# Four graph layers on one core: the statistics of x moved to the ranking loop, and three of eight source one-hots given to VectorE

## The reference

```python
h = jnp.maximum(_layernorm(x, axis=-1), 0.0)
x = x + _L0_gnn_ref(h, src, dst, ...)      # degrees of src and dst, h * norm_src @ W1, sums over edges, twice
...
# layer 0
deg_out = segment_sum(ones, src); deg_in = segment_sum(ones, dst)
norm_src, norm_dst = rsqrt(max(deg_out, 1)), rsqrt(max(deg_in, 1))
h = x * norm_src[:, None] @ W
agg = segment_sum(take(h, src), dst)
return agg * norm_dst[:, None] + b
```

## Time and profile before

| | us |
|---|---|
| median of 3 runs | 5414.27 (5409.69 to 5419.62) |
| the profiled execution | 5407.06, span 5405.3 |
| counting loop | 43 to 381 |
| ranking loop | 422 to 921 |
| first walk over the edges | from 994 |

### The profile page before, as it was taken

The page is one execution under the profiler, slowest core; times in us unless marked ns, Lnnn a source line. Parts: engine busy times, 40 slices in busy tenths (PEclk is TensorE's granted clock), DMA queues, the critical chain, the costliest instruction groups (busy, mean ns, idle before and its releaser), DMA issues. The chain is left out here.

```text
span 5405.3 us, 128432 instructions
## 1 busy us (share of the span) xinstructions
PE 4108.1 (76%) x23475; PEld 3077.4 (57%) x23476; DVE 3370.8 (62%) x11882; ACT 2977.7 (55%) x6277; POOL 3087.2 (57%) x3244
## 2 busy tenths in 40 slices
PE   3556777677668887677479999997888357777777
PEld 1124444477557776666467777776777245555555
DVE  6887776566357775677433333336877337777777
ACT  6974554377446665677433333335766236556556
POOL 0006776477765575767643345535567577777771
PEclk9899999899889998788689999999999669999999
DMA  2223333377545554788544444446888456666664
GB/s 74 76 61 92 104 104 94 117 218 217 165 139 168 167 182 147 225 266 269 170 130 135 135 136 143 145 141 216 275 277 274 143 146 201 200 199 202 202 197 148
DMA packets 599046, 905.03 MB, mean 167 GB/s; under 512 B 98280, under 2 KB 253680, under 8 KB 598956
## 3 DMA queue, kind: packets, MB, share of 16 engines
q1 hardware_dynamic: 456314, 646.24, 35.7%
q0 software_dynamic: 100352, 180.83, 13.7%
q10 hardware_dynamic: 42290, 77.00, 4.3%
HBM read 491.22 MB, written 412.49 MB: 167 GB/s over the span
## 5 line engine op out<-in xcount | busy, mean ns | idle before, releaser
L991 PE MATMUL banks<-M,OH 128*128 x9408 | 1422.4, 308 | 435.2 <-POOLq L600 224.5
L991 PEld LDWEIGHTS banks<-M,OH 128*128 128x128 f32 x9408 | 1286.2, 211 | 496.4 <-issue 471.7
L571 POOL DMA_INDIRECT M<-table_a,six x1176 | 1125.0, 957 | 472.9 <-issue 321.8
L571 POOL DMA_INDIRECT M<-table_b,six x784 | 785.4, 1002 | 671.6 <-PE banks L991 441.7
L660 ACT ACTIVATE AG<-banks x1176 | 634.3, 590 | 774.5 <-PE banks L991 737.8
L566 POOL DMA_INDIRECT edges_by_block<-pack,pos_i x392 | 376.4, 960 | 547.9 <-DVE pos_i L1213 437.7
L681 ACT ACTIVATE HO<-H,BI,SC 128x128 f32 (+1 forms) x1176 | 484.1, 482 | 292.1 <-DVE BI L1373 272.3
L660 ACT ACTIVATE T<-banks 128x512 f32<-128x512 f32 (+1 forms) x588 | 295.7, 520 | 505.0 <-PE banks L922 236.0
L1326 DVE TENSOR_TENSOR OH<-banks,dstrel 128x1024 f32<-128x1024 f32 x392 | 478.8, 1222 | 131.6 <-PE banks L991 119.4
L571 POOL DMA_INDIRECT M<-table_pairs,dix x392 | 398.9, 1018 | 119.5 <-issue 98.1
L660 ACT ACTIVATE HT<-banks 128x512 f32<-128x512 f32 x686 | 407.3, 594 | 94.1 <-PE banks L907 87.5
(11 more groups left out here) (291 smaller groups left out, 7806.4 us busy)
## 6 DMA issues: line engine op xcount, KB each, us to landing
XB<-state SPq DMA_DIRECT2D x490, 256.0 KB, 2.9
table_a<-T SPq DMA_DIRECT2D x294, 256.0 KB
state<-T SPq DMA_DIRECT2D x294, 256.0 KB
state<-H SPq DMA_DIRECT2D x196, 256.0 KB
h_turned<-HT ACTq DMA_DIRECT2D x196, 256.0 KB
table_pairs<-T SPq DMA_DIRECT2D x98, 512.0 KB
M<-messages SPq DMA_DIRECT2D x98, 512.0 KB
XB<-in_x SPq DMA_DIRECT2D x194, 256.0 KB
```

The source lines that it names most:

```text
L571: nc.gpsimd.indirect_dma_start(out=M[:, slot, :], out_offset=None, in_=table, in_offset=bass.IndirectOffsetOnAxis(ap=idx, axis=0)).then_in ...
L991: last = mm(banks[:, ds(sums_at[k], P)], OH[:, b * US + k, :], source[:, ds(rows_at[k], P)], start=False, stop=False, skip_group_check=True)
```

## The change

The statistics of x leave the counting loop. SP loads each group of x only once, in the ranking loop, into a buffer of four groups (`rows_of`, which uses XB and Z as one). There VectorE makes the statistics at lag 2 and ScalarE the deviation at lag 3; VectorE makes reciprocal, scale and offset at lag 4, each put between two of the four ranks. ScalarE norms at lag 5, TensorE turns at 6, ScalarE copies at 7, TensorE multiplies at 8 and ScalarE copies T at 9 (before, the lags on ScalarE were 3, 4 and 5, on TensorE 1 and 2). Each of VectorE's own steps waits on a mark made in an earlier step of the slot.

In the counting loop VectorE makes the source one-hots of one column in four for even groups and of two in four for odd ones (`by_vector`), as true one-hots into a bank of their own (`ps[4]`), which is added at the end. `pack` is filled with one copy from `edge4`, built once in the set-up.

```diff
@@ -185,7 +185,7 @@
...
 
-        XB = sb("XB", [P, 2, W4]); Z = sb("Z", [P, 2, W4]); HO = sb("HO", [P, 2, W4]); HT = sb("HT", [P, 2, W4])
+        XZ = sb("XZ", [P, 4, W4]); XB = XZ[:, 0:2, :]; Z = XZ[:, 2:4, :]; HO = sb("HO", [P, 2, W4]); HT = sb("HT", [P, 2, W4])
         T12 = sb("T12", [P, 2, 2, W4]); T1 = T12[:, :, 0, :]; T2 = T12[:, :, 1, :]; src2T = sb("src2T", [P, TILES], I32)
...
@@ -198,9 +198,8 @@
...
         oh_lo = tmp("oh_lo", [P, 4, P], F16); oh_hi = tmp("oh_hi", [P, 4, BLOCKS], F16)
-        sg_lo = tmp("sg_lo", [P, 4, P], F16)
+        sg_lo = tmp("sg_lo", [P, 4, P], F16); edge4 = tmp("edge4", [P, TILES, 4], I32)
         steps_c = tmp("steps_c", [P, BLOCKS]); steps_d2 = tmp("steps_d2", [P, BLOCKS]); dmat = tmp("dmat", [P, P])
-        mvx = tmp("mvx", [P, BLOCKS, 2])
         oh_bk = tmp("oh_bk", [P, 2 * CH, BLOCKS], F16)
...
@@ -229,7 +228,7 @@
...
         sg_hi = oh_bk[:, CH:2 * CH, :]
-        sdx, scx, bix = steps_d2, steps_c, dclamp
+        scx, bix = steps_c, dclamp
         early.close()
...
@@ -244,9 +243,9 @@
...
 
...
         s_pad = sem("padding_set"); s_w = sem("weights_loaded")
-        s_oh = sem("hist_onehots"); s_hist = sem("hist_columns")
+        s_oh = sem("hist_onehots"); s_so = sem("source_onehots"); s_hist = sem("hist_columns")
         s_deg = sem("degrees_read"); s_cnt = sem("block_counts")
...
@@ -274,10 +273,10 @@
...
 
-        ONE = {"pre": [0] + [1] * 6, "var": [1, 0, 1, 1, 0, 1, 1], "sd": [0, 0, 1, 1, 0, 1, 1], "ho": [1, 1, 1, 1, 0, 1, 0], "tr": [1] * 7, "ht": [1] * 7,
+        ONE = {"pre": [1] * 7, "var": [1, 0, 1, 1, 0, 1, 1], "sd": [1, 0, 1, 1, 0, 1, 1], "ho": [1, 1, 1, 1, 0, 1, 0], "tr": [1] * 7, "ht": [1] * 7,
                "mm": [1, 1, 1, 0, 1, 1, 1], "t1": [1, 1, 1, 0, 1, 1, 0], "t2": [0, 0, 1, 0, 1, 1, 0],
                "row": [0, 0, 1, 1, 0, 1, 0], "mma": [0, 0, 0, 0, 1, 0, 1], "hid": [0, 0, 0, 0, 1, 0, 1]}
-        TURN = {"in": [32, 16, 16, 16, 16, 16, 32], "late": [0, 0, 0, 0, 16, 0, 16], "st": [16] * 7,
+        TURN = {"in": [16, 16, 16, 16, 16, 16, 32], "late": [0, 0, 0, 0, 16, 0, 16], "st": [16] * 7,
                 "sv": [0, 16, 16, 16, 16, 16, 0], "sh": [0, 0, 0, 16, 0, 16, 0]}
...
@@ -309,6 +308,15 @@
...
             return AG[:, ds(k * (2 * W4) + b * W4, W4)]
+
+        def rows_of(i, b):
+
+            k = i % 2
+            return XZ[:, :, :].rearrange("p k d -> p (k d)")[:, ds(k * (2 * W4) + b * W4, W4)]
+
+        def by_vector(b):
+
+            return CH - 1 - b
 
...
@@ -377,20 +385,16 @@
...
 
-            def rows_for(free):
-
-                def do(i, b):
-                    load0(i, b, free)
-                return do
-
-            def load0(i, b, free):
-                g = 2 * i + b
-                need(sp, free, g - 1)
+            def load0(i, b):
+                g = 2 * i + b
+                need(sp, s_ho, g - 3)
+                stand(sp)
+                need(sp, s_var, g - 1)
                 stand(sp)
                 if isinstance(g, int) and g == FULL:
-                    sp.dma_start(XB[0:REST, b, :], rest(0)).then_inc(in_[b], 16)
+                    sp.dma_start(rows_of(i, b)[0:REST, :], rest(0)).then_inc(in_[b], 16)
                     return
-                sp.dma_start(XB[:, b, :], rows(a["x"], g)).then_inc(in_[b], 16)
+                sp.dma_start(rows_of(i, b), rows(a["x"], g)).then_inc(in_[b], 16)
 
...
@@ -401,11 +405,10 @@
...
 
-            staggered(sp, [(1, rows_for(s_var))])
             sp.wait_ge(s_dgc, 1)
...
 
-            staggered(sp, [(1, store0)])
+            staggered(sp, [(1, load0), (9, store0)])
             for k in range(2):
...
@@ -663,16 +666,13 @@
...
                     g = 2 * i + b
-                    if d == 0:
-                        act.wait_ge(in_[b], i * 16 + (TURNS * 16 + 16))
-                    else:
-                        act.wait_ge(s_pre, g + (at(d, "pre") + 1))
+                    act.wait_ge(s_pre, g + (at(d, "pre") + 1))
                     need(act, s_tr, g + (at(d, "tr") - 1))
...
                     for j in range(Q4):
-                        cell = q(Z4(i, b) if d in (2, 3, 5) else src_[:, b, :])[:, j, :]
+                        cell = q(rows_of(i, b) if d == 0 else Z4(i, b) if d in (2, 3, 5) else src_[:, b, :])[:, j, :]
                         if d == 0:
...
@@ -746,7 +746,7 @@
...
                 g = 2 * i + b
-                for c in range(CH):
+                for c in range(by_vector(b)):
                     col = g * CH + c
...
@@ -757,20 +757,10 @@
...
             for t in (nsrc, nsr, ndr):
-                nc.scalar.activation(t[:, :], t[:, :], ACT.Sqrt)
-            nc.scalar.activation(sdx[:, :], mvx[:, :, 1], ACT.Sqrt, bias=epsc[:, 0:1]).then_inc(s_pow, 1)
-            act.wait_ge(s_norm, 1)
-
-            def rows0(i, b):
-                g = 2 * i + b
-                need(act, s_ho, g - 1)
-                stand(act)
-                if isinstance(g, int) and g == FULL:
-                    act.dma_start(XB[0:REST, b, :], a["x"][FULL * W4:NODES].rearrange("(p j) d -> p (j d)", j=Q4)).then_inc(in_[b], 16)
-                    return
-                act.dma_start(XB[:, b, :], rows(a["x"], g)).then_inc(in_[b], 16)
-
-            staggered(act, [(5, product(0)), (4, turned(0)), (3, normed(0, XB)), (1, rows0)])
+                last = nc.scalar.activation(t[:, :], t[:, :], ACT.Sqrt)
+            last.then_inc(s_pow, 1)
+
+            staggered(act, [(3, deviations(0, (s_pre, at(0, "pre")))), (9, product(0)), (7, turned(0)), (5, normed(0, None))])
             act.wait_ge(s_rel, 1)
...
@@ -829,15 +819,19 @@
...
 
-            for k in range(2):
+            for k in (0, 1, 4):
                 mm(ps[k][:, 0:BLOCKS], zero_h[:, 0:P], oh_bk[:, 0, :], start=True, stop=False, skip_group_check=True)
...
                 g = 2 * i + b
+                mine = by_vector(b)
                 for c in range(CH):
...
                     mm(ps[1][:, 0:BLOCKS], oh_lo[:, c, :], oh_hi[:, c, :], start=False, stop=False, skip_group_check=True)
-                    pe.wait_ge(s_sg, g * CH + (c + 1))
-                    mm(ps[0][:, 0:BLOCKS], sg_lo[:, c, :], sg_hi[:, c, :], start=False, stop=False, skip_group_check=True).then_inc(s_hist, 1)
+                    if c < mine:
+                        pe.wait_ge(s_sg, i * 5 + (b * 3 + c + 1))
+                    else:
+                        pe.wait_ge(s_so, i * 3 + (b + c - mine + 1))
+                    mm(ps[0 if c < mine else 4][:, 0:BLOCKS], sg_lo[:, c, :], sg_hi[:, c, :], start=False, stop=False, skip_group_check=True).then_inc(s_hist, 1)
 
...
@@ -928,7 +922,7 @@
...
 
-            staggered(pe, [(0, ranked), (2, products(0, w1[:, :])), (1, turn_rows(0, HO))])
+            staggered(pe, [(0, ranked), (8, products(0, w1[:, :])), (6, turn_rows(0, HO))])
             pe.wait_ge(s_t1, GROUPS)
...
@@ -1050,8 +1044,7 @@
...
             v.memset(dhi[:, TILES:TILES + 1], 0.0)
-            for k in range(2):
-                v.memset(pack[k][:], 0)
+            v.memset(edge4[:, :, 3], 0)
             dve.wait_ge(s_const, 6)
...
@@ -1071,6 +1064,8 @@
...
             link(v.tensor_tensor(dst_o[:], cut_i[:], cut_j[:], ALU.bitwise_or))
+            for f, t in enumerate((src_o[:, :], dst_o[:, :], ew_o[:, :].bitcast(I32))):
+                v.tensor_copy(edge4[:, :, f], t)
             v.tensor_scalar(slo[:], slo[:], -1.0, 0.5, ALU.mult, ALU.add)
...
@@ -1110,14 +1105,11 @@
...
                     v.tensor_scalar(oh_hi[:, c, :], iota_h[:, :], dhi[:, ds(col, 1)], None, ALU.is_equal).then_inc(s_oh, 1)
-
-            def pre0(i, b):
-                g = 2 * i + b
-                dve.wait_ge(in_[b], i * 16 + 16)
-                link(spread(0, b, XB[:, b, :]))
-                v.tensor_copy(mvx[:, ds(g * Q4, Q4), :], MV[:, b, :, :]).then_inc(s_var, 1)
-
-            staggered(dve, [(0, hist), (1, pre0)], chain, 2)
+                    if c >= by_vector(b):
+                        v.tensor_scalar(sg_lo[:, c, :], iota_h[:, 0:P], slo[:, ds(col, 1)], 0.5, ALU.add, ALU.is_equal)
+                        v.tensor_scalar(sg_hi[:, c, :], iota_h[:, :], shi[:, ds(col, 1)], 0.5, ALU.add, ALU.is_equal).then_inc(s_so, 1)
+
+            staggered(dve, [(0, hist)])
             dve.wait_ge(s_hist, TILES)
...
@@ -1133,7 +1125,7 @@
...
             link(v.tensor_tensor(dego[:, 0:1], steps_d2[:, 0:1], steps_d2[:, BLOCKS - 1:BLOCKS], ALU.add))
-            link(v.tensor_scalar(dego[:, :], dego[:, :], 0.25, None, ALU.mult))
+            link(v.scalar_tensor_tensor(dego[:, :], dego[:, :], 0.25, ps[4][:, 0:BLOCKS], ALU.mult, ALU.add))
             dve.sem_inc(s_deg, 1)
...
@@ -1189,30 +1181,64 @@
...
             dve.wait_ge(s_pow, 1)
-            link(v.reciprocal(nsrc[:, :], nsrc[:, :]))
             v.reciprocal(nsr[:, :], nsr[:, :])
             v.reciprocal(ndr[:, :], ndr[:, :])
-            link(v.reciprocal(scx[:, :], sdx[:, :]))
-            link(v.tensor_tensor(scx[:, :], scx[:, :], nsrc[:, :], ALU.mult))
```

(60 more changed lines are left out.)

## The result

The changed kernel takes 5296.7 us (median, 5294.3 to 5298.5) against 5416.8 us for the kernel before on the same chip (5409.7 to 5419.6): a ratio of 0.978, 95% interval 0.977 to 0.9795. The forecast was 5322 us and its range began at 5299, so the sign was right and the gain, 120 us instead of 92, lay beyond the range. The profiled execution took 5294.3 us, 112.8 us less than the one of before.

A forecast was written before the change was run, and what follows sets the result against it. ScalarE was taken to bound the counting loop, POOL's stores the ranking loop. Counting -110, set-up +1.1, between loops -3.7, ranking +8, drain +12 gave -92 us: 5322 us against the median 5414.27, range 5299 to 5367.

The forecast's parts named there:

- the new bound: Counting loop: VectorE becomes the bound, 11 one-hot pairs at 0.395 us, 4.35 us per pair of groups, 49 times.
- the 1 us of end: Counting loop: 1 us added at its end, after VectorE's 49 pairs of groups.
- the 10.2 us in which its loop turns show as issue: Counting loop: VectorE's issue time at loop turns, 10.2 us, added to its time once it is the bound.
- I take 4 us: Counting loop: loss to TensorE's low clock, 4 us, cutting the gain from 114 to 110 us.
- Rival 2: Counting loop: TensorE bounds it at the low clock, 5.2 us per pair of groups; 5350 us, chance 0.10.
- The three copies: Before the counting loop: three copies of 392 elements build `edge4`, 0.36 us each, +1.1 us.
- the undisturbed slot: Ranking loop: a slot of 3.74 us where VectorE waited for nobody; with the added work about 5.0 us.
- the mean slot: Ranking loop: estimate from VectorE's mean slot, 4.04 us; with the added work 5.3 us.
- rival 1: Ranking loop: VectorE bounds it for good, 5.4 us a slot, costing 30 instead of 8 us; 5344 us, chance 0.23.
- Rival 3: Ranking loop: loads come late, slower than before; 5510 us if loads take 8.5 us, chance 0.05.
- the sign of a lock: Ranking loop: one-hots at 351 against 317 ns read as VectorE and GpSimd locking each other out of SBUF.
- Rival 5: Both loops and drain: no low clock, ranking loop stays with POOL, drain 9; -108 us, 5306 us, chance 0.09.

The follow-up runs named there:

- the repeat: The changed kernel timed once more, unedited, beside the kernel before: 5292.9 against 5409.9 us, ratio 0.978.
- the kernel with its own wait: The changed kernel plus a VectorE wait for its own last source one-hot after each pair of groups in the counting loop: 5315.9 us.

## Why the prediction was wrong

The measured 5296.7 us lie 25.3 under the forecast and 2.3 under its range. Of the 25.3, 20.7 are between the profiled execution (5294.3) and the 5315 forecast for it. The other 4.6 are the step from there to the median: 7 us were added, as in the kernel before, and the medians of the changed kernel lie 2.4 us above its own profiled execution, and at it in the repeat.

**What bounds the kernel** was read rightly in both loops: ScalarE's pace in the counting loop (with all signs it takes 6.4 us a pair of groups, to the digit), POOL's in the ranking loop, and 1 us of slack there: the kernel before took in 78 us of added work for 3 us of time.

**Counting loop.** The price of a source pair, 0.395 us against 0.393 measured, the new bound and the 1 us of end held: 49 x 4.35 = 213 us, measured 212.1, and 0.95 for the end. What failed is the step between them, "plus the 10.2 us in which its loop turns show as issue, hidden until now behind ScalarE". That term measured nothing. The idle time was read as a property of the turn, when it was one of a turn behind a drained engine, and what had drained it, the statistics' waits on themselves, was just what the change removes. This one term is 10 of the 20.7 us.

**The clock.** "I take 4 us" should have been nothing: the grant was 1.00 from 43 to 253 us. Rival 2, TensorE at the low clock, did not occur. The forecast's "its pauses of some 2 us during the statistics vanish" came true, but that the grant rose for this reason is argued and not shown: the kernel before, with its pauses, was granted 1.00 from 60 to 110 us too. The Trainium skill, "TensorE: Matmul & The Clock Gate", section "Part 1: The HAM clock gate", would have given that 0, and the trace agrees with it here.

**Set-up.** The three copies cost 0.1, not 1.1 us: they fell into the time in which VectorE waited for the weights' transpose.

**Ranking loop.** +2.7 us where 8 were taken (5.17 us a slot). VectorE's waits and issue gaps are 46 us, so its own work is some (502 - 46) / 98 = 4.65 us a slot, under the "about 5.0" from the undisturbed slot and well under the 5.3 of the mean slot and the 5.2 of rival 1. Adding recorded durations overstates this engine; the distances of starts (0.09 us for an operation on 128x4, about 0.2 for a bn_stats) do not. The waits on its own results were rightly priced at nothing, but only because rank steps stand between them, which the prediction named as a queue and not as the condition: 85 us hang on it. Rival 3's loads were never late in the loop. The forecast also took the one-hots' 351 ns against 317 for the sign of a lock; recorded durations don't bear that out, since in the counting loop, where GpSimd does nothing, the same shape was recorded at means of 331 and 540 ns in two executions of the changed kernel. The rule cited in the forecast from the Trainium skill, "SBUF — State Buffer", section "Who interferes with whom", gave 0 here and the measured 2.7 lies near it; no run here isolates the lock itself.

**Drain.** 19.4 us against 17: right to 2 us. The loads that arrive late there (2.4 us in two waits) were not in the sum. It priced a slot of drain at some 2.8 us; one slot less of lag took off 4.6.

**Range.** Rival 5, the sum of all the good ends, stood at 5306, and the range went 7 us below it, to 5299. But rival 5 too held the 10.2 us of turns, as did every case in which VectorE bounds the counting loop. Without them it would have stood at 5296. The comparison itself gave 4 to 7 us more than the profiled executions do.

## What to carry to other kernels

Work that can't be made cheaper may still be worth moving: find the stage where its engine has measured slack (here 1.05 us a slot in front of a store's buffer), pay it there, and let the freed engine take over a part of its neighbour's work (here three pairs in eight) in the other stage; each half alone brought 18 us or cost 51. Where an instruction depends on the one before it on the same engine, put independent work between; where two engines hand over, a slot between them costs up to 4.6 us once, in the drain, and its lack can cost 2 us in every slot. An idle time seen in an engine that is not the bound is no term of the sum for the time when it becomes one, until it is clear what had caused it; and what follows a drain serially can often be issued inside it.

## What the runs showed of the hardware that was not expected

- VectorE's recorded durations are no measure of its pace. In the changed kernel's counting loop a pair of one-hots is 0.393 us apart from the first to the last, yet the wide one is recorded at 0.32 us at 45 us and at 0.75 in the last pair. In the repeat of the same kernel, at the same distance, the mean hardly grows. These are the groups of the two executions, 60 to 250 us, and of the kernel with its own wait:

```profile
L1107 DVE TENSOR_SCALAR oh_hi<-iota_h,dhi 128x392 f16<-128x392 f16 x352 | 156.6, 540 | 0.0
```

```profile
L1107 DVE TENSOR_SCALAR oh_hi<-iota_h,dhi 128x392 f16<-128x392 f16 x351 | 116.2, 331 | 0.0
```

```profile
L1107 DVE TENSOR_SCALAR oh_hi<-iota_h,dhi 128x392 f16<-128x392 f16 x316 | 100.8, 319 | 0.0
```

  The 319 ns of the third can't be put down to the wait, since the second has 331 without one. What makes the durations grow in one execution and not in another stays open.
- TensorE busy 32 of 50 us in an even stream was granted 1.00, that is 2.4 GHz; busy 30 of 50 us with pauses of 2.4 us and more it was granted 0.70, a mix of 2.4 and 1.2 GHz. The kernel before had both 1.00 and 0.73 with one and the same rhythm, so the pauses alone do not say which it will be.
- A turn of the loop cost VectorE nothing visible in an unbroken stream, 0.26 us on top of a wait for its own last result, and 0.38 us behind a single short copy.
